# Gram tiles 0 and 1 computed together, other orders on every engine up to the first pass, and the first selection rounds of tiles 6 and 7 moved into pass 0

## What is computed

```
# level 0: 8 nearest neighbours of each point, then 4 blocks
d2 = sq[:, :, None] + sq[:, None, :] - 2.0 * einsum('bdn,bdm->bnm', xyz, xyz)
_, idx = top_k(-d2, 8)
for i in range(4):
    p = leaky_relu(points, 0.01)
    c  = einsum('oi,bin->bon', w_center[i], p)
    gn = einsum('oi,bikn->bokn', w_neighbor[i], gather(p, idx))
    points = (c + gn.sum(axis=2)) / 9.0 + points
# level 1: 30 nearest neighbours, a small network on their first three coordinates,
# a softmax over the 30, and the weighted sum of their features
idx = top_k(2 * x_loc @ x_loc.T - |.|^2 - |.|^2, 30)
att = softmax(mlp_with_batch_norm(relative_coordinates(idx)))
out = x + einsum('bnkc,bnk->bnc', x[idx], att)
```

## Time and profile before

| | before |
|---|---|
| time, median of 3 runs | 791.47 us (790.16 to 792.34) |
| time of the profiled execution | 791.82 us |
| its span, first to last instruction | 789.9 us |
| PE busy | 742.2 us (94%) |
| DVE busy | 631.9 us (80%) |
| ACT busy | 254.7 us (32%) |
| POOL busy | 204.0 us (26%) |
| mean granted clock of TensorE | 0.972 |
| chain that ended last, by engine | PE 71%, DVE 17%, ACT 4%, issue 3%, POOL 3% |

### The profile page before, as it was taken

The page is one execution under the profiler, slowest core; times in us unless marked ns, Lnnn a source line. Parts: engine busy times, 40 slices in busy tenths (PEclk is TensorE's granted clock), DMA queues, the critical chain, the costliest instruction groups (busy, mean ns, idle before and its releaser), DMA issues.

```text
span 789.9 us, 13131 instructions
## 1 busy us (share of the span) xinstructions
PE 742.2 (94%) x5530; PEld 604.1 (76%) x5530; DVE 631.9 (80%) x943; ACT 254.7 (32%) x415; POOL 204.0 (26%) x158
## 2 busy tenths in 40 slices
PE   5879899798999999999999999898899898999998
PEld 4668788776778887888878888686687787777776
DVE  4777999949999999999998789867754877778741
ACT  7325553521363121210010344433444233333220
POOL 3112867780321301301220161450262000000000
PEclk9989999989999999999999999999999999999999
DMA  9620003001002000255442000000000000010101
GB/s 356 180 106 2 1 1 107 1 28 80 1 0 101 8 2 2 78 175 178 152 152 77 1 1 0 1 0 1 0 1 1 1 1 2 28 41 29 41 27 54
DMA packets 21179, 39.87 MB, mean 50 GB/s; under 512 B 10112, under 2 KB 10112, under 8 KB 20864
## 3 DMA queue, kind: packets, MB, share of 16 engines
q1 hardware_dynamic: 20976, 36.93, 13.4%
q10 hardware_dynamic: 144, 2.10, 0.7%
HBM read 32.59 MB, written 6.42 MB: 49 GB/s over the span
## 4 chain that ended last, share of the span: by engine, by line
PE 71%; DVE 17%; ACT 4%; issue 3%; POOL 3%; DMA 1%; SPq 0%; POOLq 0%; DVEq 0%; ACTq 0%
PE bank L1425 26%; PE bank L1449 5%; PE bank L1560 4%; PE bank L1404 4%; PE bank L1405 4%; PE bank L1406 4%; PE bank L1510 4%; PE bank L1561 4%; PE bank L1562 4%; PE bank L1323 3%; PE bank L1324 3%; PE bank L1325 3%; DVE pts_l L920 2%; DVE idx L848 2%; DVE vals L846 2%
## 5 line engine op out<-in xcount | busy, mean ns | idle before, releaser
L1425 PE MATMUL bank<-nbr,pts_l 128*128 128x512 f32 x1024 | 246.8, 400 | 7.5 <-DVE pts_l L920 7.3
L1425 PEld LDWEIGHTS bank<-nbr,pts_l 128*128 128x128 f32 x1024 | 194.6, 192 | 51.1 <-DVE pts_l L920 10.4
L462 POOL TENSOR_TENSOR pts_h<-scratch,pts_h 128x512 fp32r<-128x512 f32 x58 | 78.8, 1364 | 166.3 <-ACT pts_h L657 166.3
L1404 PE MATMUL bank<-wT,pts_h 128*128 128x512 f32 x256 | 105.4, 412 | 8.9 <-DVE pts_l L920 4.8
L1405 PE MATMUL bank<-wT,pts_h 128*128 128x512 f32 x256 | 102.8, 402 | 0.0
L1406 PE MATMUL bank<-wT,pts_h 128*128 128x512 f32 x256 | 102.4, 400 | 0.0
L1323 PE MATMUL bank<-pts_h 128*128 128x512 f32 (+2 forms) x192 | 72.8, 379 | 14.2 <-DVE pts_l L819 10.5
L664 ACT CAST pts_l<-bank 128x512 fp32r<-128x512 f32 x64 | 37.5, 588 | 138.6 <-PE bank L1406 138.5
L657 ACT CAST pts_h<-scratch 128x512 fp32r<-128x512 f32 x58 | 35.6, 616 | 131.2 <-DVE scratch L915 127.4
L1324 PE MATMUL bank<-pts_l,pts_h 128*128 128x512 f32 (+2 forms) x192 | 69.3, 361 | 0.0
L1325 PE MATMUL bank<-pts_h,pts_l 128*128 128x512 f32 (+2 forms) x192 | 69.2, 360 | 0.0
(11 more groups left out here) (205 smaller groups left out, 1249.9 us busy)
## 6 DMA issues: line engine op xcount, KB each, us to landing
more<-a_rows SPq DMA_DIRECT2D x17, 480.0 KB, 4.4
scratch<-a_rows SPq DMA_DIRECT2D x15, 480.0 KB, 4.2
X<-in_ctx SPq DMA_DIRECT2D x12, 512.0 KB, 6.5
out_dram<-X SPq DMA_DIRECT2D x16, 256.0 KB, 2.0
more<-in_ctx SPq DMA_DIRECT2D x4, 512.0 KB, 7.0
scratch<-in_fside_BxSxS SPq DMA_DIRECT2D x2, 1024.0 KB, 12.4
w_keep<-wT SPq DMA_DIRECT2D x1, 2048.0 KB, 6.3
X<-in_x SPq DMA_DIRECT2D x2, 1024.0 KB, 6.7
```

What stands on the lines that cost most here:

```text
L462: pool.tensor_tensor(p_l[:, t, hf * HALF:(hf + 1) * HALF], p32(n), p_h[:, t, hf * HALF:(hf + 1) * HALF].bitcast(F32), ALU.subtract).then_i ...
L1404: pe.matmul(bank[g % 3][:], p_h[:, t, cols], wT[:, 0, t, :], start=(t == 0), stop=False)
L1425: mm = pe.matmul(bank[3 + g % 3][:], y[:, m, t * P:(t + 1) * P], nbr[b][:, m, hf * HALF:(hf + 1) * HALF], start=(m == 0 and part_ == 0), s ...
```

## The change

PE computes tiles 0 and 1 of image 0 stage by stage together (`first_grams`), before `norms(0)`. The turned blocks of tiles 0 and 1 are made inside `gram(2)`, those of tile 2 late in `gram(3)` (`TURN_IN`). The lists of ACT, DVE, POOL and PE up to the first pass have other orders. The adjacency of tiles 6 and 7 goes to step 1 of pass 0 (`ADJ_AT[1]`). `side(0)` on DVE gets nine selection rounds in place of two; six of these are the rounds 0 to 2 of tiles 6 and 7 that stood ahead of pass 0. On DVE `low_half` moves from tile 3 to tile 2, and `tab` from ahead of `p_make` to behind the last round of tiles 4 and 5. Nothing is computed differently.

The core of the diff:

```diff
+    TURN_IN = {2: {(0, KT - 1): 0, (1, 4): 1}, 3: {(1, 4): 2}, NT: {}}
...
-        STEP_LIST = [(T, n) for n in range(3, STEPS) for T in (6, 7)] \
+        STEP_LIST = [(T, n) for n in range(STEPS) for T in (6, 7)] \
...
+        STEPS_AT = (2, 2, 2, 2, 2, 2, 2, 2, 2, 2, 2, 2, 2, 2, 2, 2)
+            n = STEPS_AT[g % 16] + (7 if g == 0 else 0)
+        ADJ_AT[1] = (6, 7)
@@ POOL
-            diagonal(2)
             for k in range(KT):
                 low_part(k, 0)
+            diagonal(2)
             add_norm(4)
-            diagonal(3)
             for k in range(4):
                 low_part(k, 1)
+            for k in range(1, 3):
+                add_square(KT + k)
             add_norm(5)
-            for k in range(1, 4):
+            diagonal(3)
+            for k in range(3, KT):
                 add_square(KT + k)
+            add_norm(6)
+            add_norm(7)
             diagonal(4)
...
-            for T in range(NT, 11):
-                add_norm(T)
...
             for n in range(CT):
                 p_low(n)
-            diagonal(6)
-            diagonal(7)
-            add_norm(11)
-            add_norm(12)
+            for T in range(NT, 13):
+                add_norm(T)
@@ ACT, ahead of the first pass
-            mirror_out(14)
-            adjacency(6)
-            adjacency(7)
+            for T in range(13, TILES - 1):
+                gram_out(T)
+                mirror_out(T)
             gram_out(15)
             for j in range(CT, 2 * CT):
                 p_high(j)
-            nbr_out(6)
-            nbr_out(7)
@@ DVE
-            select([0])
+            select([0], 0, 9)
             for n in range(CT):
                 w_low(n)
+            select([0], 9)
             select([1])
-            select([2], 0, 6)
+            select([2], 0, 5)
             for n in range(CT, 2 * CT):
                 w_low(n)
-            select([2], 6)
-            select([3], 0, 3)
+            select([2], 5, 9)
             for k in range(4, KT):
                 low_half(k)
-            select([3], 3)
-            select([4, 5])
+            select([2], 9)
+            select([3])
...
+            select([4, 5], 0, 5)
             for n in range(CT):
                 p_make(n)
-            select([6, 7], 0, 3)
+            select([4, 5], 5, 8)
             for n in range(CT, 2 * CT):
                 p_make(n)
+            select([4, 5], 8)
@@ PE
+            def first_grams():
+                for k in range(KT):
+                    pe.wait_ge(s_pl0, k + 1)
+                    for T in range(2):
+                        for c0, c1, o in PIECES[T]:
+                            mm = product(T, k, c0, c1, o)
+                        if k == KT - 1:
+                            mm.then_inc(s_g, 1)
...
-            gram(0)
+            first_grams()
             norms(0)
-            gram(1)
+            gram(2)
             for n in range(CT):
                 w_turn(n)
-            gram(2)
+            gram(3)
             adj_turn(0)
-            gram(3)
             gram(4)
...
-                if g == 1:
-                    adj_turn(6)
-                    adj_turn(7)
                 for T in ADJ_AT.get(g - 1, ()):
                     adj_turn(T)
```

110 lines of the change are left out of this document (47 added, 63 removed).

## The result

The changed kernel takes 772.38 us, median of 4 runs (771.8 to 773.01), where the kernel before, run beside it, takes 791.29 us (790.16 to 792.34, 4 runs). The ratio is 0.9761, 95% interval 0.9744 to 0.9778. The profiled execution took 771.8 us, with a span of 769.8 us, 20.1 less than before.

A forecast was written before the change was run, and what follows sets the result against it. PE bounds the kernel, losing time in the front; after the change POOL's late diagonals hold pass 0, leaving 9.3 us. 791.8 less 9.3 is 782.5, the median 0.3 lower: 782.2 us; range 776 to 788.5.

The forecast's parts named there:

- The front on PE: PE up to the first `wp`: 18.6 us of waits and half clock gone, 1.05 + 1.7 added; grams end 15.9 us earlier.
- the first step: PE, tiles 0 and 1 together: eight stages until 30.0; 3.7 us idle and 1.7 us of half clock gone.
- The next thing that is late is POOL: `adj_turn(6)` behind `wp(2)` waits for POOL's diagonal, giving PE a new idle of 16 us.
- tab: DVE ahead of pass 0: five instructions held by POOL's adds, 8.6 us beyond their own 2.15; bounds 0 and 10.
- DVE is hidden: Pass 0: `y_low(3)` could start at 166.1 but `y_high(3)` comes at 168.4, so DVE is hidden behind POOL by 2.3 us.
- Rival 1: POOL's chain does not bind, `aggregate(0)` ends 11 to 19 us earlier, with luck 25: 767 to 776; chance 0.05.
- POOL's chain: POOL from 130.6 us: `p_low`, `add_norm` and two diagonals take 31.0 us, `diagonal(7)` at 161.6.
- Rival 4: Slower: DVE and POOL collide in `p_make(4..7)` too, 8.6 us, up to 796 us; chance 0.08.
- `low_half` collision: Before `gram(8)`: two of DVE's four `low_half` meet POOL's `add_square`; last comes 4.8 us later, PE 1.7 us later.
- 5.5 us of activity at half clock: PE behind the new idle before `adj_turn(6)`: half clock over 5.5 us active, costing 2.7 us.
- In the later passes selection is one round ahead, which I count at nothing: Passes after pass 0: selection one round ahead, counted at nothing.

The follow-up runs named there:

- e4_grams_apart: Kernel after with only the inner order of `first_grams` put back, tile 0 over all its stages and then tile 1; 777.73 us.
- e2_diag_early: Kernel after with diagonal(6) and diagonal(7) on POOL moved ahead of add_norm(13..15); 772.55 us.
- e3_both: Kernel after with `tab` at step 13 of pass 0 and, on POOL, p_low(4..7) and both diagonals ahead of the last six add_norm; 764.68 us.
- e1_tab_moved: Kernel after with DVE's five `tab` instructions moved from ahead of pass 0 to its step 13; 771.59 us.
- a_shift_small: Kernel after with SP's first load held until seven of POOL's constants are made, order unchanged; 778.73 us.
- a_shift_large: Kernel after with SP's first load held until eleven of POOL's constants are made, order unchanged; 779.61 us.

## Why the prediction was wrong

**Right, by its own steps.**
- *The front on PE.* First grams to the end at 30.0: as forecast, with no wait for a load. Tile 0's selection at 35.2: 35.13. `w_low` in time: no wait. `adj_turn(2)` waits 1.05: 1.28. `gram(8)` at 75.7: 75.2. e4_grams_apart gives the first step its price: 5.4 us in the medians, 6.3 in the trace. The grams end at 135.6, not 137.3.
- *The next thing that is late is POOL.* One idle of 14.3 us (forecast 16) before `adj_turn(6)`, released by the diagonal at 158.5 (161.6). e2_diag_early and e3_both bear out the reason, the diagonals' place in the queue.
- *tab.* 9.95 us in total; my term was 2.15 and 8.6, so 10.75. And that DVE is hidden by some 2.3 us: 1.57. e1_tab_moved confirms that it costs nothing here, and e3_both that time comes out when both engines are relieved.
- *The page.* By the Trainium skill, "SBUF — State Buffer", section "Who interferes with whom", a cast in a two-port mode or a DVE instruction with two SBUF inputs, and POOL's add, which reads SBUF, exclude one another for a whole instruction. Two subtractions and two casts of 2.3 us each beside adds of 2.4, and 0.2 us without them, agree.
- *Rivals.* Rival 1, a front gain that stays whole, gave 767 to 776, and the time fell in there; but its mechanism didn't occur: POOL's chain did bind. (Its own 11 to 19 us less would be 772 to 780; the 767 needed the 25.) The time alone would have misled here. Rival 4 didn't occur: `p_make(4..7)` ran from 124.3 to 126.8, ahead of POOL's start at 129.16, in 2.6 us.

**Wrong: the sum at the end of pass 0, by 3.8 us** (13.1 at `aggregate(1)` against 9.3). Its terms had the right sign, and three were too dear:
- POOL starts at 129.16, not 130.6: 1.4 us. The first full clock came at 11.8 us and not at 12.5, and the `low_half` collision cost PE 1.0 us, not 1.7. DVE's part was nearly as priced, 4.4 us (6.93 in place of 2.49) against 4.8.
- POOL's chain took 29.4 us, not 31.0: 1.6 us. I gave it 1.0 us of loss to `tab`; five `add_norm` took 11.8 us, as without any loss. Each `tab` instruction waited for an add, not the add for it.
- Behind the idle I took 5.5 us of activity at half clock, from the earlier trace rows; it was 3.7 (158.19 to 161.9), worth 0.9 us. The other work from there to the update behind `aggregate(1)` took 0.5 us longer than walked, and `adj_turn(6)` began 0.3 us ahead of the end of both diagonals, on which I had put it.

**Wrong: that the later passes stay as they are, 6.7 us.** "In the later passes selection is one round ahead, which I count at nothing" was all that I said of them, and it is true of the work: the idles are equal to 0.03 us. The step of the prediction that failed is this one: I carried the clock of passes 1 to 7 over from the trace of before, as if it were part of the work, and so put at nothing a term that came out at 6.7 us. With the 3.8 us alone the time would have been some 778.4, inside my range; the 6.7 took it out. The earlier trace rows had it in view: a clock of 0.98 in the stretch from 189.9 to 350 us, which meant a loss; that anything upstream can move it, the runs showed. A small shift brings most of it back: the spans of a_shift_small and a_shift_large are 7.9 and 7.4 us longer than that of the kernel after, of which 2.8 and 2.2 us were there at the end of pass 0, so 5.1 and 5.2 us were lost in the later passes.

**What stays open.** Why the kernel before lands at 0.970 to 0.976 in 39 of 44 executions beside these runs (788.95 to 793.7 us) and at 0.983 to 0.987 in the other five (783.6 to 786.3), while the kernel after is at 0.985 to 0.989. That it is the place of idles in time is shown for single stretches. That this place is what separates the two kernels in every execution is argued: only one execution of each has a trace. Nor is it shown that the 6.7 us belong to this change: a shift of 2 us took most of them away, so I call them luck. Against those five quicker executions of the kernel before, the median of the kernel after is 11.3 to 13.9 us shorter.

## What to carry to other kernels

When an engine's wait goes, look in the queue of the engine that is late next for the instruction that is really waited for, and at the same time at the engine that is hidden just behind it: here relieving DVE alone gave nothing, two diagonals earlier on POOL gave nothing in the time, and relieving both engines gave 7.7 us. A short instruction on DVE beside a run of POOL's adds was priced by the adds here, 2.3 us and not 0.2. Where the trace of before has short half-clock stretches behind idles of 0.8 to 2 us, put them into the range on both sides, at up to 1.6 us each: an edit upstream can add or remove them.
